# Post-norm attention with product-key experts on one core: another order of preparation, attention outputs paired, 24 maxima ahead instead of 28, one norm two maxima later

## The chip, the core and the metric

The kernel runs on one core of a Trainium2 chip. Its engines work side by side and wait for one another through semaphores: PE (TensorE) multiplies matrices, DVE (VectorE), ACT (ScalarE) and POOL (GpSimd) work elementwise, and SP (SyncE) issues all of the DMAs here, on one queue. The metric is device time in microseconds (us), the median of some runs. The profiled execution is one further run with its own time.

## What is computed

Cut to what matters, for 4 sequences ("batches") of 512 tokens, width 128, 16 heads of width 8, 32 experts:

```python
q, k, v = split_heads(x @ Wq), split_heads(x @ Wk), split_heads(x @ Wv)
attn = softmax(q @ k.T * e ** -0.5) + rel_table[rel_index].reshape(h, s, s)   # per head
x = layernorm(x + (layernorm_1e-3(attn @ v) * gamma + beta))
sim = (x @ hasher_w.T) @ keys.T
vals, idx = top_k(sim, 4);  w = softmax(vals)
o = sum_k w_k * (silu(x @ values_down[idx_k]) @ values_up[idx_k])
out = layernorm(x + (x + o * scale))
```

## The kernel before, in words

**Exactness by pieces.** Queries and keys are needed more exactly than bf16 holds, so each is split into three bf16 pieces (`parts`: high, middle, low). The high one is a copy of the product, `resid` is what is left of it, the middle one a copy of `resid`, the low one `resid` minus the middle one. The pieces go to DRAM (`write_parts`, six DMAs for a batch) and come back as stacks of 72 rows per head (`load_slice`, two DMAs for a group of four heads), `q_stack` and `k_stack`. A score is then one matmul over the 128 rows of both stacks.

**Softmax shift.** The shift of each query, the negative maximum of its row of scores, must be known before the exponentials. For a head and a chunk of 128 queries PE computes scores into one of two banks `sm_ps` (L1003), DVE reduces them (`maximum`, L746). I call the pair "a maximum". There are 64 for a batch, 16 for a group of four heads. When the 16 of a group are done, POOL splits them in three (`split_shift`, L392 to L399), PE turns them (job `shift1` and so on), ACT copies them to `shift_rows` and one DMA lays them into rows 96 to 98 of `q_stack` (`load_shift`).

**Rounds and positions.** Round t (0 to 3) does attention of batch t in 16 positions u, four to a group of heads. A position holds four scores matmuls (L1014), four exponentials on ACT (L645), four maxima for a position 7 ahead (`LEAD`), and the products with the values of the position before (L1027, four per position, stationary `v_cur`). In rounds 1 to 3 the norms, the routing and the experts of batch t-1 are done between them, in rounds 2 and 3 the last part (`up`) of batch t-2 too, and a tail without attention follows.

**Who orders the work.** Nobody plans it: the order of each engine is written out by hand. The table `JOBS` gives for each position the jobs that PE does before and behind its last score; ACT, with `copies`, follows the same table, and DVE has its own places (u, s), where s counts the four maxima of a position. Each engine runs its own list in order and stops at the first wait that isn't met.

**Outputs.** After the four positions of a group, ACT copies the bank `ov_ps` to `o_sb` (`o_copy`), PE turns it by four transposes (jobs `o0` to `o3`, L1032), and DVE divides by the sums (`attend`: a reciprocal at L765 and a multiplication at L767). A head's weights in `v_cur` are 32 columns wide, of which 8 hold values, one holds ones for the sum, and the others zeros.

**Preparation.** `prep(b)` does the transposes of x, the products with the three weights, with three banks of PSUM. PE does `prep(0)` to `prep(2)`, then two maxima, then `prep(3)`, the tables of the relative bias and 28 maxima in all (`EARLY`) between them before round 0.

Of the kernel before, what the change touches and what calls it, by code (L numbers as in the profile page):

```python
# [5 lines left out]
def bass_postln_attention_product_key_ffn(nc, x, w_q, w_k, w_v, rel_table, gamma, beta,  # L6
# [16 lines left out]
    FJ = NE // NJ  # L23
    TOPK = 4
# [5 lines left out]
    EARLY = LEAD * C  # L30
# [16 lines left out]
    with ctx:  # L47
# [36 lines left out]
        rsum = sb("rsum", [P, C, J])  # L84
# [35 lines left out]
        consts_made, stack_set = sem("consts_made"), sem("stack_set")  # L120
# [5 lines left out]
        first_split, mid_made, low_made = sem("first_split"), sem("mid_made"), sem("low_made")  # L126
# [22 lines left out]
        def maxima_of(u, more):  # L149

            return [(u + LEAD, c) for c in range(C) if more or u + LEAD < U]

        JOBS = {0: (["up0", "up1"], ["o3"]), 1: (["up2", "up3"], []), 2: (["shift1", "up4"], ["up5"]),
# [5 lines left out]
        OWN = ("shift0", "shift1", "shift2", "shift3", "o0", "o1", "o2")  # L159
        SPREAD = tuple(f"w{j}" for j in range(FJ))  # L160
        SIDE = ("o0", "x1t", "sim", "o1", "wt", f"up{FJ - 1}") + SPREAD
# [23 lines left out]

        def jobs_of(kind):
            return [n for u in sorted(JOBS) for half in JOBS[u] for n in half if here(n, *kind)]

# [47 lines left out]
        ACT_STEPS = ["tanh0", "sexp"] + [f"tanh{j}" for j in range(1, FJ)]  # L236
# [46 lines left out]
        def _(sp):  # L283
# [35 lines left out]
            def write_parts(b, heads, written):  # L319

                for a in range(2):

                    sp.wait_ge(*((first_split, 2 * a + 2) if b == 0 else (low_made, split_count(b, a))))
# [9 lines left out]
            sp.wait_ge(stack_set, 2)  # L333
# [49 lines left out]
        def _(pool):  # L383
# [17 lines left out]
            def fetch_values(t, g):  # L401

                if not is0(t):

                    pool.wait_ge(pv_done, (t - 1) * U + C * (g + 1))
                    apart(pool)
                nc.gpsimd.tensor_copy(v_cur[:, :, g * J:(g + 1) * J, 0:D],  # L407
                                      v_all[:, :, g * J:(g + 1) * J, t, :]).then_inc(v_ready, 1)
# [59 lines left out]
            nc.gpsimd.memset(q_stack[64:P].bitcast(F32), 0.0).then_inc(stack_set, 1)  # L468
            pool.wait_ge(stack_set, 2)
# [6 lines left out]
            nc.gpsimd.memset(v_cur[:, :, :, D:D + 1], 1.0).then_inc(consts_made, 1)  # L476
            for i in range(PARTS):
                rows = slice(i * NE, (i + 1) * NE)
                pool.wait_ge(consts_made, 8)
                if i:  # L480
                    pool.wait_ge(spread_made, i)
                nc.gpsimd.tensor_copy(spread[rows], ident[rows, rows].rearrange("r (j n) -> r j n", j=FJ).unsqueeze(3)
                                      .to_broadcast([NE, FJ, NJ, PD])).then_inc(spread_made, 1)
            pool.wait_ge(spread_made, PARTS)
# [8 lines left out]
            for g in range(G):  # L493
                fetch_values(0, g)
            low_parts(B - 1)
            split_shift(0, 0)

            def round_(t, attention, experts, more, late):
# [3 lines left out]
                if experts and attention:  # L502

                    pool.wait_ge(misc_done, job(t, "o3", is_kept))
# [55 lines left out]
        def _(act):  # L560
# [3 lines left out]
            def middle_parts(b):  # L564

                for a in range(2):
                    act.wait_ge(resid_made, 2 * b + a + 1)
                    copy(parts[:, b, a, 1, :], resid[:, b % 2, a]).then_inc(mid_made, 1)
# [695 lines left out]
```

## Time and profile before

| | us |
|---|---|
| median of 3 runs (339.32 to 341.76) | 341.53 |
| the profiled execution, its own time | 340.26 |
| its span, first to last instruction | 338.4 |
| PE busy | 303.5 (90%) |
| DVE busy | 237.6 (70%) |
| ACT busy | 202.6 (60%) |
| POOL busy | 127.8 (38%) |
| mean granted clock of TensorE, share of full speed | 0.974 |

The span falls in a preparation of 46.7 us, round 0 (to about 99.8), round 1 (to about 164.5), round 2 (to about 232.7), round 3 (to about 294.1) and a tail of 44.3 us. Busy time of PE overlaps itself, since matmuls are pipelined: a matmul with 512 columns in bf16 shows 380 ns, and the next one can start 0.22 us after it. An engine's idle time counts only where another one waits for what comes late. A row of the timeline may merge neighbours of one kind (x4), and some that overlap a cut are shown twice.

### The profile page before, as it was taken

What the parts mean: (1) busy time and instruction counts of PE and PEld (TensorE: products, weight loads), DVE (VectorE), ACT (ScalarE), POOL (GpSimd) and SP (SyncE); (2) the same over time, 40 slices, a digit from 0 to 9 for tenths busy, and PEclk for the clock granted to TensorE, in tenths of its full rate; (3) what the DMA queues carried; (4) which work ended last, traced back from release to release, by engine and by line L of the source; (5) the groups of instructions that cost most, each with busy time, mean ns of one, the idle gap of its engine ahead of it and who ended that gap; (6) DMA issues with size and microseconds to landing.
All of it is one profiled execution on the core that took longest, in us unless ns stands there. A gap on an engine that the chain in (4) does not pass through costs nothing. (4 is left out here: it accounts for less than half of the span.)

```text
span 338.4 us, 5001 instructions
## 1 busy us (share of the span) xinstructions
PE 303.5 (90%) x1671; PEld 127.8 (38%) x1671; DVE 237.6 (70%) x525; ACT 202.6 (60%) x396; POOL 127.8 (38%) x204
## 2 busy tenths in 40 slices
PE   4859989999999799999998999999989999768890
PEld 2534332332232243333653433335544332465280
DVE  0836897888789869878568798786677922275733
ACT  2544266676776667798455677985556799502600
POOL 8975100100106621164355511653555026324121
PEclk9998999999999999999999999999999999995997
DMA  5486970279520202020202130202001000001001
GB/s 158 104 244 161 302 196 4 71 264 287 153 71 3 71 4 71 1 70 6 69 1 70 35 70 2 73 1 72 1 0 35 0 2 2 0 2 31 0 0 31
DMA packets 28230, 23.17 MB, mean 68 GB/s; under 512 B 6526, under 2 KB 26670, under 8 KB 28206
## 3 DMA queue, kind: packets, MB, share of 16 engines
q1 hardware_dynamic: 28206, 22.87, 24.6%
q8 instruction: 13, 0.21, 0.3%
q14 instruction: 11, 0.09, 0.1%
HBM read 12.18 MB, written 10.52 MB: 67 GB/s over the span
## 5 line engine op out<-in xcount | busy, mean ns | idle before, releaser
L746 DVE TENSOR_REDUCE neg_max<-sm_ps 128x1 f32<-128x512 f32 x256 | 167.8, 684 | 44.9 <-PE sm_ps L1003 43.9
L645 ACT ACTIVATE probs<-st_ps 128x512 f32<-128x512 f32 x256 | 138.4, 612 | 43.0 <-PE st_ps L1014 43.0
L1003 PE MATMUL sm_ps<-k_stack,q_stack 96*128 96x512 bf16 x256 | 98.3, 385 | 9.4 <-DVE neg_max L746 4.5
L1014 PE MATMUL st_ps<-q_stack,k_stack 128*128 128x512 bf16 x256 | 86.3, 380 | 0.7 <-ACT probs L645 0.7
L1027 PE MATMUL ov_ps<-probs,v_cur 128*32 128x512 f32 x512 | 68.2, 605 | 0.5 <-ACT probs L645 0.5
L1003 PEld LDWEIGHTS sm_ps<-k_stack,q_stack 96*128 96x128 bf16 x256 | 24.6, 97 | 103.3 <-DVE neg_max L746 84.7
L435 POOL TENSOR_TENSOR hid<-hid,w_rows 128x512 f32<-128x512 f32 x26 | 33.1, 1273 | 39.1 <-ACT w_rows L562 33.7
L1014 PEld LDWEIGHTS st_ps<-q_stack,k_stack 128*128 128x128 bf16 x256 | 25.3, 99 | 24.9 <-ACT probs L645 6.8
L1048 PEld LDWEIGHTS si_ps<-up_sb,hid 128*128 128x128 f32 x256 | 30.6, 192 | 1.0
L1048 PE MATMUL si_ps<-up_sb,hid 128*128 128x128 f32 x256 | 31.0, 276 | 0.0
L1108 PE MATMUL mi_ps<-x_t,down_sb 128*128 128x512 f32 x48 | 24.8, 598 | 0.3 <-ACT shift_rows L562 0.3
L801 DVE SCALAR_TENSOR_TENSOR hid<-tanh_sb,mi_ps 128x512 f32<-128x512 f32 x24 | 16.3, 681 | 12.1 <-ACT tanh_sb L682 12.1
L682 ACT ACTIVATE tanh_sb<-mi_ps 128x512 f32<-128x512 f32 x24 | 14.6, 608 | 10.4 <-PE mi_ps L1108 10.1
L407 POOL COPY v_cur<-v_all 128x128 f32<-128x128 f32 x16 | 4.5, 289 | 41.1 <-PE ov_ps L1027 41.1
L1027 PEld LDWEIGHTS ov_ps<-probs,v_cur 128*32 128x32 f32 x512 | 10.1, 108 | 22.6 <-issue 17.1
L392 POOL CAST shift_parts<-neg_max 128x16 bf16<-128x16 f32 x16 | 3.1, 196 | 39.9 <-DVE neg_max L746 28.5
L562 ACT ACTIVATE w_rows<-si_ps 128x512 f32<-128x512 f32 x24 | 15.2, 632 | 1.7 <-PE si_ps L1113 1.7
L562 ACT ACTIVATE o_sb<-ov_ps 128x512 f32<-128x512 f32 x16 | 9.7, 606 | 5.3 <-PE ov_ps L1027 5.1
L777 DVE BATCH_NORM_STATS2 stats<-z 128x6 f32<-128x128 f32 x32 | 7.5, 281 | 6.7 <-POOL z L520 6.7
L416 POOL TENSOR_SCALAR veps<-mv 128x4 f32<-128x4 f32 x8 | 1.8, 225 | 26.8 <-DVE mv L786 19.3
L562 ACT ACTIVATE x_t<-si_ps 128x512 f32<-128x512 f32 x4 | 2.4, 598 | 14.7 <-PE si_ps L1032 14.7
L1108 PE MATMUL st_ps<-x_t,down_sb 128*128 128x512 f32 x16 | 10.2, 782 | 0.3 <-DVE hid L801 0.3
(143 smaller groups left out, 295.1 us busy)
## 6 DMA issues: line engine op xcount, KB each, us to landing
stack_dram<-parts SPq DMA_DIRECT2D x18, 384.0 KB, 4.4
q_stack<-stack_dram SPq DMA_DIRECT2D x16, 288.0 KB
k_stack<-stack_dram SPq DMA_DIRECT2D x16, 288.0 KB
stack_dram<-parts SPq DMA_DIRECT2D x6, 288.0 KB, 5.0
x_sb<-L_attn_x SPq DMA_DIRECT2D x4, 256.0 KB, 3.2
out<-y_out SPq DMA_DIRECT2D x4, 256.0 KB, 2.5
stack_dram<-parts SPq DMA_DIRECT2D x6, 96.0 KB, 2.0
down_sb<-L_ffn_values_down SPq DMA_DIRECT2D x1, 512.0 KB, 7.6
```

Source lines behind the costliest of these rows:

```text
L435: nc.gpsimd.tensor_tensor(hid[:, j], hid[:, j], w_rows[:, j], ALU.mult).then_inc(weighed, 1)
L562: return nc.scalar.activation(dst, src, ACT.Copy, scale=scale)
L645: nc.scalar.activation(probs[:, u % 2, j, :], st_ps[:, score_bank(u * J + j), :], ACT.Exp, scale=SCORE_SCALE).then_inc(probs_ready, 1)
L682: nc.scalar.activation(tanh_sb[:, j % 3, :], down_bank(t, j), ACT.Tanh, scale=0.5).then_inc(act_step, 1)
L746: nc.vector.tensor_reduce(neg_max[:, g % 2, col:col + 1], sm_ps[:, c % 2, :], AX.X, ALU.max, negate=True).then_inc(max_ready, 1)
L777: i = nc.vector.bn_stats(into[:, c, :], src[:, c, :])
L801: nc.vector.scalar_tensor_tensor(out=hid[:, j], in0=tanh_sb[:, j % 3, :], scalar=1.0, in1=down_bank(t, j), op0=ALU.add, op1=ALU.mult).then ...
L1003: nc.tensor.matmul(sm_ps[:, c % 2, :], q_stack[0:SHIFT_ROW, h, c * P:(c + 1) * P], k_stack[0:SHIFT_ROW, h, :], start=True, stop=True).then ...
L1014: nc.tensor.matmul(st_ps[:, score_bank(k), :], k_stack[:, g * J + j, kc * P:(kc + 1) * P], q_stack[:, g * J + j, :], start=True, stop=True ...
L1027: i = nc.tensor.matmul(ov_ps[j * TILE:(j + 1) * TILE, :], v_cur[:, kc, g * J + j, :], probs[:, u % 2, j, :], start=(kc == 0), stop=(kc == ...
L1048: i = nc.tensor.matmul(si_ps[:, c * P:(c + 1) * P], hid[:, j, c * P:(c + 1) * P], up_sb[:, j, :], start=(j == 0 and c == 0), stop=(j == FJ ...
L1108: i = nc.tensor.matmul(down_bank(t, j), down_sb[:, j * NJ:(j + 1) * NJ, :], x1_t[:], start=True, stop=True)
```

## The change

Five things change.

1. **Preparation.** DVE clears the lower half of `q_stack` (POOL did). The middle pieces of batch 0 are made by ACT (DVE did), and both low ones follow on DVE. The remainders of batch 3 are copied by ACT and subtracted by POOL (DVE subtracted them straight from PSUM). POOL makes `spread` at its end of the preparation. PE does the transposes of batch 3 ahead of its first two maxima.
2. **SP's queue.** The first `load_shift` goes ahead of `gamma`, `scale` and the pieces of batch 1.
3. **Pairs.** Groups 2n and 2n+1 share one accumulation in `ov_ps`: the even group has values in columns 0 to 7 and the sum in 8, the odd one in 16 to 23 and 24. There are 2 output jobs for a batch, `o0` at position 8 and `o1` in the next round's position 0, for 4 before. `attend` has one reciprocal of 128x32 and two multiplications.
4. **24 maxima ahead.** The positions 0 to 3 of round 0 hold five maxima each.
5. **Round 1.** The statistics of the second norm stand two maxima later, and `x1t` stands in position 6 ahead of `shift2`, with `sim` behind the last score.

The order of PE in the preparation, from the third `prep` on (`x_sb` is the input, `sm_ps` a maximum). Before:

```order
L976 MATMUL st_ps<-ident,x_sb 128x128 x4
L985 MATMUL st_ps<-x_t,wq_sb 128x512
L986 MATMUL st_ps<-x_t,wk_sb 128x512
L990 MATMUL st_ps<-wv_sb,x_t 128x128 x4
L1003 MATMUL sm_ps<-k_stack,q_stack 128x512 x2
L976 MATMUL ov_ps<-ident,x_sb 128x128 x4
L1003 MATMUL sm_ps<-k_stack,q_stack 128x512
L985 MATMUL mi_ps<-x_t,wq_sb 128x512
L986 MATMUL si_ps<-x_t,wk_sb 128x512
```

And now:

```order
L997 MATMUL st_ps<-ident,x_sb 128x128 x4
L1006 MATMUL st_ps<-x_t,wq_sb 128x512
L1009 MATMUL st_ps<-x_t,wk_sb 128x512
L1013 MATMUL st_ps<-wv_sb,x_t 128x128 x4
L997 MATMUL ov_ps<-ident,x_sb 128x128 x4
L1026 MATMUL sm_ps<-k_stack,q_stack 128x512 x2
L1006 MATMUL mi_ps<-x_t,wq_sb 128x512
L1026 MATMUL sm_ps<-k_stack,q_stack 128x512
L1009 MATMUL si_ps<-x_t,wk_sb 128x512
```

The transposes of batch 3 have moved ahead of the first two maxima, and one maximum stands between its two products.

SP's queue at the same place, behind the loads of the last slice (`shift_rows` is the shift of group 0). Before:

```order
L339 DMA gamma_sb<-L_attn_gamma 128x128
L340 DMA scale_sb<-L_ffn_scale 128x1
L327 DMA stack_dram<-parts 384x1x512 x3
L327 DMA stack_dram<-parts 128x1536 x3
L298 DMA q_stack<-shift_rows 3x16x128
L343 DMA down_sb<-L_ffn_values_down 128x32x32
```

And now:

```order
L307 DMA q_stack<-shift_rows 3x16x128
L350 DMA gamma_sb<-L_attn_gamma 128x128
L351 DMA scale_sb<-L_ffn_scale 128x1
L336 DMA stack_dram<-parts 384x1x512 x3
L336 DMA stack_dram<-parts 128x1536 x3
L353 DMA down_sb<-L_ffn_values_down 128x32x32
```

The shift has moved ahead of eight DMAs. The expert loads stand ahead of the shift of group 1, as before.

DVE in round 1, from the first norm's last step to the routing's first. Before:

```order
L786 BN_AGGR mv<-stats 128x2 x4
L746 TENSOR_REDUCE neg_max<-sm_ps 128x1 x7
L777 BN_STATS stats<-z 128x6 x2
L746 TENSOR_REDUCE neg_max<-sm_ps 128x1
L777 BN_STATS stats<-z 128x6 x2
L746 TENSOR_REDUCE neg_max<-sm_ps 128x1
L786 BN_AGGR mv<-stats 128x2 x4
L746 TENSOR_REDUCE neg_max<-sm_ps 128x1 x2
L765 RECIPROCAL rsum<-si_ps 128x16
L767 TENSOR_TENSOR attn<-si_ps,rsum 128x4x32
L746 TENSOR_REDUCE neg_max<-sm_ps 128x1 x7
L863 MAX top<-sim 128x8 x4
```

And now:

```order
L808 BN_AGGR mv<-stats 128x2 x4
L769 TENSOR_REDUCE neg_max<-sm_ps 128x1 x9
L799 BN_STATS stats<-z 128x6 x2
L769 TENSOR_REDUCE neg_max<-sm_ps 128x1
L799 BN_STATS stats<-z 128x6 x2
L769 TENSOR_REDUCE neg_max<-sm_ps 128x1
L808 BN_AGGR mv<-stats 128x2 x4
L769 TENSOR_REDUCE neg_max<-sm_ps 128x1 x8
L885 MAX top<-sim 128x8 x4
```

Nine maxima stand ahead of the statistics instead of seven, and the output's two instructions are gone from here (they come at position 10).

The diff, cut to its core:

```diff
-    EARLY = LEAD * C
+    EARLY = (LEAD - 1) * C
...
-        def maxima_of(u, more):
+        def maxima_of(t, u, more):
+            if t == 0 and u < C:
+                return [divmod(k, C) for k in range(EARLY + u * (C + 1), EARLY + (u + 1) * (C + 1))]
             return [(u + LEAD, c) for c in range(C) if more or u + LEAD < U]
-        JOBS = {0: (["up0", "up1"], ["o3"]), 1: (["up2", "up3"], []), 2: (["shift1", "up4"], ["up5"]),
-                3: (["up6"], ["up7"]), 4: ([], ["o0"]), 5: ([], ["x1t"]),
-                6: (["shift2", "sim"], ["down0"]), 7: ([], ["down1"]), 8: ([], ["o1", "down2"]),
+        JOBS = {0: (["up0", "up1"], ["o1"]), 1: (["up2", "up3"], []), 2: (["shift1", "up4"], ["up5"]),
+                3: (["up6"], ["up7"]), 4: ([], []), 5: ([], ["x1t"]),
+                6: (["shift2", "sim"], ["down0"]), 7: ([], ["down1"]), 8: ([], ["o0", "down2"]),
...
-                12: (["w2"], ["down6", "w3"]), 13: (["w4"], ["down7", "w5"]), 14: (["shift0", "w6"], ["o2"]),
+                12: (["w2"], ["down6", "w3"]), 13: (["w4"], ["down7", "w5"]), 14: (["shift0", "w6"], []),
+        SHORT_JOBS = {**JOBS, 5: ([], []), 6: (["x1t", "shift2"], ["sim", "down0"])}
...
+            load_shift(0, 0)
             sp.dma_start(gamma_sb[:], bass.AP(gamma.tensor, 0, [[0, P], [1, E]])).then_inc(rows_loaded, 16)
             sp.dma_start(scale_sb[:], bass.AP(ffn_scale.tensor, 0, [[0, P], [1, 1]])).then_inc(rows_loaded, 16)
             write_parts(1, slice(0, H), parts_written[1])
-            load_shift(0, 0)
...
+            for a in range(2):
+                pool.wait_ge(last_copied, a + 1)
+                nc.gpsimd.tensor_sub(resid[:, 1, a], resid[:, 1, a], parts[:, B - 1, a, 0, :]).then_inc(last_resid, 1)
+            split_shift(0, 0)
             low_parts(B - 1)
-            split_shift(0, 0)
+            for i in range(PARTS):
...
                     copy(parts[:, b, a, 0, :], made).then_inc(prep_copied, 1)
+                    if b == B - 1:
+                        act.wait_ge(low_made, split_count(b - 2, a))
+                        copy(resid[:, 1, a], made).then_inc(last_copied, 1)
+                if b == 0:
+                    middle_parts(0)
...
-                    if u == 7 and experts:
+                    if u == 8 and experts:
                         act.wait_ge(pool_step, pool_at(t - 1, "sdiff"))
...
+            nc.vector.memset(q_stack[64:P].bitcast(F32), 0.0).then_inc(rows_cleared, 1)
...
-                        nc.vector.tensor_copy(parts[:, b, a, 1, :], resid[:, 0, a]).then_inc(first_split, 1)
...
-                nc.vector.reciprocal(rsum[:], o[:, :, :, D]).then_inc(rsum_ready, 1)
-                dve.wait_ge(rsum_ready, n + 1)
...
+                nc.vector.reciprocal(rsum[:], o[:, :, :, :, D]).then_inc(rsum_ready, 1)
+                dve.wait_ge(rsum_ready, t * PAIRS + n + 1)
+                for k in range(2):
+                    g = 2 * n + k
+                    i = nc.vector.tensor_tensor(attn[:, :, g * J * D:(g + 1) * J * D].rearrange("p c (j d) -> p c j d", d=D),
+                                                o[:, :, :, k, 0:D], rsum[:, :, :, k].unsqueeze(3).to_broadcast([P, C, J, D]),
+                                                ALU.mult)
...
-                elif at == ((3, 1) if late else (4, 0)):
+                elif at == ((3, 1) if late else (4, 2)):
...
-                        if attention and s == 0 and u in (5, 9, 15):
+                        if attention and (u, s) == (10, 1):
...
                 for j in range(J):
                     i = nc.tensor.matmul(ov_ps[j * TILE:(j + 1) * TILE, :], v_cur[:, kc, g * J + j, :],
-                                         probs[:, u % 2, j, :], start=(kc == 0), stop=(kc == C - 1))
+                                         probs[:, u % 2, j, :], start=(g % 2 == 0 and kc == 0),
+                                         stop=(g % 2 == 1 and kc == C - 1))
```

## Rows read from the trace of the kernel before

**Rows 1.** The page, part 1 and part 5 (columns: busy us, mean ns, idle before).

```profile
PE 303.5 (90%) x1671; PEld 127.8 (38%) x1671; DVE 237.6 (70%) x525; ACT 202.6 (60%) x396; POOL 127.8 (38%) x204
...
L562 ACT ACTIVATE o_sb<-ov_ps 128x512 f32<-128x512 f32 x16 | 9.7, 606 | 5.3 <-PE ov_ps L1027 5.1
```

**Rows 2.** Windows by stage: busy time per engine, PE's clock, DMA share, GB/s.

```profile
46.70:99.80 53.10, 52.62 (x281) 15.22 (x279) 43.83 (x75) 38.07 (x76) 4.42 (x20) 1.00 0.47 143
99.80:164.50 64.70, 62.14 (x334) 22.40 (x334) 52.74 (x115) 46.73 (x94) 26.53 (x44) 1.00 0.17 41
164.50:232.70 68.20, 66.67 (x381) 28.25 (x380) 54.15 (x123) 46.93 (x92) 29.75 (x48) 1.00 0.16 40
```

**Rows 3.** Timeline of the first 19 us: start, length, engine, line, tiles, idle before.

```profile
9.10 1.64 DVE L730 CAST parts<-resid 128x512 bf16<-128x512 f32 x1
10.77 0.69 DVE L732 TENSOR_TENSOR parts<-resid,parts 128x512 bf16<-128x512 f32 x1
11.49 4.36 SPq L327 DMA_DIRECT2D stack_dram<-parts  x6
11.82 3.65 POOL L482 CAST spread<-ident 32x1024 bf16<-32x1024 f32 x3
13.17 1.40 DVE L732 TENSOR_TENSOR parts<-resid,parts 128x512 bf16<-128x512 f32 x1
15.56 3.72 POOL L489 TENSOR_TENSOR x_sb<-x_sb,beta_sb 128x512 f32<-128x512 f32 x3
16.04 1.13 PE L985 MATMUL st_ps<-x_t,wq_sb 128*128 128x512 f32 x2 [0.74 <-ACT x_t L562]
```

**Rows 4.** Timeline from 22 us to the first scores.

```profile
22.49 0.60 PE L1003 MATMUL sm_ps<-k_stack,q_stack 96*128 96x512 bf16 x2 [3.57 <-DMA k_stack<-stack_dram]
29.63 0.63 PE L1032 MATMUL st_ps<-ident,rel_win 128*128 128x128 f32 x4 [0.30 <-issue]
31.53 6.46 SPq L327 DMA_DIRECT2D stack_dram<-parts  x6
31.55 7.80 DVE L746 TENSOR_REDUCE neg_max<-sm_ps 128x1 f32<-128x512 f32 x12
39.26 0.21 PE L1032 MATMUL mi_ps<-ident_bf,shift_parts 128*128 128x128 bf16 x1 [0.63 <-POOL shift_parts L399]
44.90 0.60 ACT L562 ACTIVATE bias_v<-st_ps 128x512 f32<-128x512 f32 x1 [0.45 <-PE st_ps L1032]
```

**Rows 5.** Windows of the same stretch, columns as in Rows 2.

```profile
22.48:28.90 6.42, 6.12 (x21) 3.20 (x22) 2.58 (x4) 2.83 (x5) 4.43 (x7) 0.73 0.65 218
28.90:46.70 17.80, 15.46 (x112) 6.41 (x111) 15.57 (x25) 6.96 (x15) 3.10 (x6) 1.00 0.98 262
```

**Rows 6.** DMA issues: name, count, size, us from issue to landing.

```profile
up_sb<-L_ffn_values_up SPq DMA_DIRECT2D x1, 512.0 KB, 9.3
...
gamma_sb<-L_attn_gamma SPq DMA_DIRECT2D x1, 64.0 KB, 8.8
```

**Rows 7.** Timeline of round 0, at the end of group 0.

```profile
58.04 2.48 DVE L746 TENSOR_REDUCE neg_max<-sm_ps 128x1 f32<-128x512 f32 x4 [0.61 <-PE sm_ps L1003]
61.49 0.65 PE L1032 MATMUL si_ps<-ident,o_sb 128*128 128x128 f32 x4
61.98 0.38 PE L1014 MATMUL st_ps<-q_stack,k_stack 128*128 128x512 bf16 x1
...
63.44 0.25 DVE L765 RECIPROCAL rsum<-si_ps 128x16 f32<-128x16 f32 x1
63.72 0.29 DVE L767 TENSOR_TENSOR attn<-si_ps,rsum 128x128 f32<-128x128 f32 x1
```

**Rows 8.** Timeline of PE in rounds 1 and 2, where it stood idle.

```profile
114.07 0.39 PE L1003 MATMUL sm_ps<-k_stack,q_stack 96*128 96x512 bf16 x1 [1.19 <-DVE neg_max L746]
118.97 0.63 PE L1032 MATMUL si_ps<-ident,x 128*128 128x128 f32 x4 [0.91 <-POOL x L425]
180.09 0.39 PE L1003 MATMUL sm_ps<-k_stack,q_stack 96*128 96x512 bf16 x1 [0.72 <-DVE neg_max L746]
```

More of the change, by code:

```diff
@@ L184, in here, with jobs_at @@
             return (late if n[:2] == "up" else attention if n in OWN else experts) and (more or n != "shift0")
+        def jobs_at(kind, u):
+            return (SHORT_JOBS if kind == SECOND else JOBS).get(u, ([], []))
         def jobs_of(kind):
-            return [n for u in sorted(JOBS) for half in JOBS[u] for n in half if here(n, *kind)]
+            return [n for u in range(U) for half in jobs_at(kind, u) for n in half if here(n, *kind)]
         def job(t, name, counted):
@@ L235, in bass_postln_attention_product_key_ffn @@
         LATE_POOL = ["ceps", "ccentre", "cpow"]
-        ACT_STEPS = ["tanh0", "sexp"] + [f"tanh{j}" for j in range(1, FJ)]
+        ACT_STEPS = ["tanh0", "tanh1", "sexp"] + [f"tanh{j}" for j in range(2, FJ)]
         def dve_at(f, name):
@@ L406, in fetch_values @@
                     apart(pool)
-                nc.gpsimd.tensor_copy(v_cur[:, :, g * J:(g + 1) * J, 0:D],
+                first = HALF_TILE * (g % 2)
+                nc.gpsimd.tensor_copy(v_cur[:, :, g * J:(g + 1) * J, first:first + D],
                                       v_all[:, :, g * J:(g + 1) * J, t, :]).then_inc(v_ready, 1)
@@ L475, in _ @@
             nc.gpsimd.tensor_copy(ident_bf[:], ident[:]).then_inc(consts_made, 1)
[L476 to L484, printed above, removed]
+            for half in range(2):
+                sums = v_cur[:].rearrange("p c (n k j) w -> p c n k j w", n=PAIRS, k=2)[:, :, :, half]
+                last = HALF_TILE * half + D
+                for n in range(PAIRS):
+                    i = nc.gpsimd.memset(sums[:, :, n, :, last:last + 1], 1.0)
+            i.then_inc(consts_made, 1)
             pool.wait_ge(beta_loaded, 16)
@@ L693, in round_ @@
                 for u in range(U):
-                    before, behind = JOBS.get(u, ([], []))
+                    before, behind = jobs_at((attention, experts, more, late), u)
                     if attention:
@@ L839, in expert_steps @@
                 if at == (1, 0):
-                    attend(f, G - 1, t)
+                    attend(f, PAIRS - 1, t)
                     if not attention:
@@ L922, in round_ @@
                 for u in range(U):
-                    maxima = maxima_of(u, more) if attention else []
+                    maxima = maxima_of(t, u, more) if attention else []
                     for s in range(C):
-                        if s < len(maxima):
-                            maximum(t, *maxima[s])
-                        if attention and s == 0 and u in (5, 9, 15):
-                            g = {5: 0, 9: 1, 15: 2}[u]
-                            attend(t, g, t)
+                        for pos_c in maxima[s:s + 1] if s < C - 1 else maxima[s:]:
+                            maximum(t, *pos_c)
+                        if attention and (u, s) == (10, 1):
+                            attend(t, 0, t)
                         if late and attention:
@@ L1021, in values @@
                     pe.wait_ge(v_ready, t * G + g + 1)
-                    if not (is0(t) and g == 0):
-                        pe.wait_ge(o_copied, t * G + g)
+                    if g % 2 == 0 and not (is0(t) and g == 0):
+                        pe.wait_ge(o_copied, t * PAIRS + g // 2)
                 pe.wait_ge(probs_ready, J * n + J)
@@ L1071, in misc @@
                         pe.wait_ge(hidden_made, hidden_count(f, int(last[4:])))
+                    elif last == name and t == B:
+                        pe.wait_ge(hidden_made, hidden_count(f - 1, FJ - 1))
                 elif int(name[4:]) >= 3:
@@ L1121, in early_maxima @@
                         maximum_scores(0, *early.pop(0))
-            for b in range(B - 1):
+            for b in range(B):
                 prep(b)
-            early_maxima(2)
-            prep(B - 1)
             early_maxima(2)
@@ L1200, in round_ @@
                 for u in range(U):
-                    before, behind = JOBS.get(u, ([], []))
+                    before, behind = jobs_at(kind, u)
                     if not attention and u == 0:
                         before, behind = behind, before
-                    todo = maxima_of(u, more) if attention else []
+                    todo = maxima_of(t, u, more) if attention else []
                     def maxima(k):
-                        for pos_c in todo[k:k + 1]:
+                        for pos_c in todo[k:k + 1] if k < C - 1 else todo[k:]:
                             maximum_scores(t, *pos_c)
@@ L1215, in score @@
                                 scores(t, u, j)
-                    spread = not any(here(n, *kind) and n[:2] in ("do", "up") for n in JOBS.get(u - 1, ([], []))[1])
+                    spread = not any(here(n, *kind) and n[:2] in ("do", "up") for n in jobs_at(kind, u - 1)[1])
                     score(*range(1 + spread))
```

91 lines of the change are left out of this document (48 added, 43 removed).

## The prediction

> **What bounds the kernel now.** I read the page first: PE is busy 90% of the span, DVE 70%, ACT 60% [rows 1]. Then the windows by stage, since a share of the whole says nothing about a stage: in round 0 PE is busy 52.6 of 53.1 us, in round 1 62.1 of 64.7, in round 2 66.7 of 68.2, with its clock at full speed, 2.4 GHz [rows 2]. So in the rounds what counts is what PE must do and the few places where it waits. A plain position of round 0 is shared, though: DVE needs 2.48 us for its four maxima and idles 0.61 us while PE is at the value products, 3.09 us together [rows 7]. Neither can shorten it alone, and a fifth maximum lengthens it. Last, the timeline of the preparation, which is a chain and no throughput: pieces of batch 0, their write, their load, the first maximum at 22.49 us [rows 3, 4].
>
> **The preparation, step by step.** The sum is made against the profiled execution, 340.26 us (span 338.4).
>
> *First write.* SP issues the first three DMAs at 11.49 and the other three when the second low piece is ready, at 13.17 + 1.40 = 14.57; all are issued at 15.85, so three take 1.28 us [rows 3]. ACT takes over the middle pieces, which is 0.60 us each there [rows 1] for 1.64 us of a cast on DVE [rows 3]. Then the second low piece is ready at about 12.9 and the queue is free at 12.77: gain 1.7 us. The floor is 1.0 us, if a subtraction is held up once more, the ceiling 1.8 us (the queue). ACT's two copies, 0.60 us each, come ahead of the copies that `prep(1)` waits for, so batches 1 and 2 move some 0.65 us back. That hides behind the load's way, since PE waited 3.57 us for it [rows 4].
>
> Here the trace and a rule differ a little. A low piece's subtraction took 0.69 us beside POOL's memsets and 1.40 us beside its cast of `spread` [rows 3]. The new place is beside POOL's additions of beta, of 1.24 us each [rows 3]; I take 0.69 and 1.40 once more. The Trainium skill, SBUF — State Buffer, section Who interferes with whom, says that a DVE instruction with two SBUF inputs is held off by a GpSimd instruction that reads SBUF, for all of its length. By that rule both could wait for an addition, and the sum below would be some 0.7 us higher.
>
> *Batch 3.* PE stood still for 3.57 us before the first maximum, and in the 6.42 us after it its clock was 0.73 of full: part of it at half speed, 1.2 GHz [rows 4, 5]. Now the transposes of batch 3 fill most of the wait: PE's idle there shrinks to under 1 us and I expect no fall. The first maximum comes at 22.49 - 1.7 = 20.8. From it to the table transposes there were 29.63 - 22.49 = 7.1 us. Now there are six maxima at 0.22, two products of about 1.1 us at full clock [rows 3], the values' 1.1, and ACT's copy of it, some 4.7 us: the table comes at 25.5, a gain of 4.1 us (the 1.7 in it). Floor 2.5 us, if the clock falls all the same.
>
> *Shift of group 0.* DVE had done 6 maxima when its run of 12 in 7.80 us began at 31.55; the 16th was its tenth, at 38.0, and PE turned the shift at 39.26 [rows 4]. Without the last two subtractions on DVE it has 8 behind it at 27.5 and does the other 8 at 0.62 to 0.65 us by 33. The turn comes 1.3 us later, at 34.3: gain 5.0 us. POOL's two new subtractions (1.2 us each by the additions [rows 3]) are over by then, and it makes the last low pieces and `spread` (3.65 us [rows 3]) behind it, where nobody asks until round 1.
>
> *First scores.* Before they came at 46.7, behind four last maxima at 0.62 us each. These are gone, but the last bias copy, which PE waits for, ended at 45.5 [rows 4], so no more than 1.1 us is gained: scores at 40.6, **-6.1 us** in all (floor -3.5, ceiling -7). The shift's DMA, now ahead of `gamma`, has 5 us to land.
>
> **Round 0.** 16 maxima are now spread as 20 over four positions, 0.60 to 0.62 us for each extra: **+2.4 us** (ceiling; the floor is +0.9, four times PE's 0.22, if DVE's idle 0.61 took them in, but that idle lies around the value products and a maximum behind the fourth doesn't reach it). An output job costs PE 61.98 - 61.49 = 0.49 us and DVE about as much (0.25 and 0.29), and a position with one is about 0.4 us longer [rows 7]. There were three; there is one, with one more multiplication of 0.29: -0.55 us. **Round 0: +1.9 us.**
>
> **Round 1.** PE waited 1.19 us for DVE, which stood at the second norm's statistics, and 0.91 us at `x1t` for POOL [rows 8]. Two maxima later in the order DVE comes there about when POOL's result is ready, and `x1t` behind another position meets its input: -2.1. `sim` then stands only two short matmuls behind `x1t`, and must wait for ACT's copy of 0.60 us: +0.4. Two output jobs fewer, 0.44 us each on a busy PE, are -0.9, and position 8 to 9, where DVE is late, gives 0.2: **-2.8 us.** POOL's chain from `attend` to the first norm doesn't move; it starts 0.25 us later by the longer `attend`.
>
> **Rounds 2 and 3.** Their norms stay where they were; the wait at the statistics, 0.72 us [rows 8], hangs on POOL and grows by 0.25. Two output jobs and a piece of DVE's load are gone in each: -1.25 + 0.25 = **-1.0 us each**. In the second half of round 3 ACT carries the experts' copies too, and loses one of 0.60 us: **-0.4 us.**
>
> **Tail.** It waits for `attend` from its start: one multiplication more, **+0.3 us**. The rest of its 44.3 us has the same instructions.
>
> Costed at nothing: the clearing of `q_stack` on DVE (DVE has nothing to do before the first subtraction, which comes ahead of the 9.10 of its cast [rows 3]); the eight copies that ACT loses in the middle rounds (it idles between exponentials there); the exponential of the routing one position later, whose reader comes another position behind. If ACT became late, that last one would cost its 0.33 us.
>
> **Sum:** -6.1 + 1.9 - 2.8 - 1.0 - 1.0 - 0.4 + 0.3 = -9.1, so 340.26 - 9.1 = 331.2 us. The median of the runs shown is 1.3 us above that execution; I forecast a median of **332 us**.
>
> **The rivals.**
>
> *A, the start is bound by its DMAs (time 335.5, chance 0.2).* The DMA share from 28.9 to 46.7 was 0.98 [rows 5], `gamma` took 8.8 us to land behind the slices [rows 6]. If the slice of group 1 lands no earlier than before, the maxima from the 17th on wait. The same would hold if ACT, which waits for `scale` ahead of the first exponential, gets it late: it is now issued at about 36.5. Then the start gives 2.5 us instead of 6.1. Against it: the chain that fills the queue starts 1.7 us earlier as a whole, and the write of batch 1 moves out of the way.
>
> *B, the expert loads hold the shift of group 1 (334, chance 0.1).* SP now issues the write of batch 1 behind the first shift: some 34.8 + 0.9 for the shift, 1.4 for `gamma` and `scale`, 6.46 for the six writes [rows 4], so it comes to `down` and `up` at 43.5, and `up`, issued right behind `down`, took 9.3 us to land [rows 6]: 53 to 53.5. The shift of group 1 is behind both in the queue, and PE needs it at 40.6 + 4 x 3.09 + 4 x 0.6 - 0.6 = 54.8. The margin is 1 to 2 us; if it's eaten up, about 2 us are lost.
>
> *C, more than forecast (328.5, chance 0.1).* All waits of the rounds fall together: the fifth maxima cost 0.9 and the late rounds give 2 us each.
>
> *D, no change to measure (338.5 to 341, chance 0.05).* The order of the preparation doesn't do what it says: the first write gains nothing, since the landing rather than the issue decides, and the clock falls as before. Then only the rounds are left: about -3, less what A takes.
>
> *E, slower (344, chance 0.03): PE at half clock in the first four positions of round 0.* After the 3.57 us of idleness the clock was at half for a part of the next 6.42 us [rows 4, 5]. If it fell once more at the start of round 0, where PE now does 3.0 us of work in 3.7, a position would take some 6.6 us, 3 more each, and the gain of 9.1 turns to +3. It decides if the window of these positions shows a clock of 0.5. Against it: the same engine ran rounds 0 to 3 at 1.00 with waits of up to 1.19 us in them [rows 2, 8]. The Trainium skill, TensorE: Matmul & The Clock Gate, What's actually happening, has the clock follow how busy PE has been lately; by it such a fall could be, and the trace at these shares speaks against it.
>
> My forecast has the rest, 0.52, with a range of its own of 330 to 334.5.
>
> **Range and chances.** 328.5 to 337 us takes in the forecast, A, B and C, and leaves D and E out, with tails of the others. A measurement of this kernel tells a change of 1% (3.4 us) from none. Faster by over 1%, that is below 338.1: the forecast, A, B, C, 0.92. Within 1%: 0.05. Slower by over 1%: 0.03.
>
> **What would show it.** In the windows: the first scores at 40 to 41.5 us and a clock near 1.00 from 20 to 29 us; positions of 3.7 us four times, then 3.1; round 0 of about 55 us; in round 1 no wait of PE at DVE's statistics or at `x1t`, and one of about 0.4 at `sim`; rounds 2 and 3 each 1.0 to 1.4 us shorter; tail 44.6. The prediction is wrong if the first scores stay above 43 us, if a half-clock window stands in round 0, or if the fifth maximum costs much less or more than 0.6.

## The result, and the profile after

The changed kernel ran in 338.59 us (median of 20 executions, 336.26 to 341.6), the kernel before beside it in 340.57 (20 executions). The ratio is 0.9932, with a 95% interval of 0.9915 to 0.9949; it leaves out two slow executions of the changed kernel (341.32 and 341.6). So the gain is real and small, 0.7%, which is within the 1% called no change, and far from the 332 us forecast. 338.59 lies above the range (328.5 to 337) too.

The profiled execution took 337.84 us against 340.26 (spans 336.0 and 338.4), so 2.4 us less, where 9.1 were predicted. First, on the page, the busy time of each engine [rows 1 for before]:

```profile
PE 300.0 (89%) x1639; PEld 124.1 (37%) x1639; DVE 235.6 (70%) x514; ACT 200.9 (60%) x392; POOL 126.1 (38%) x208
```

The shares are those of before to a point. Where the time went is told by the windows by stage of the changed kernel (from, to, length, then busy time and count of PE, PEld, DVE, ACT, POOL, PE's clock, DMA share, GB/s), to be held against [rows 2]. A round's border is, as there and to 0.1 us, the start of the fourth exponential of its first position. Round 0 begins with its first scores, and the tail with the turn of the last output (288.9 here, 293.6 before, where the prediction's tail of 44.3 us began at 294.1):

```profile
41.70:96.40 54.70, 52.86 (x276) 14.77 (x276) 44.58 (x74) 37.11 (x74) 4.45 (x20) 1.00 0.62 181
96.40:160.20 63.80, 61.86 (x326) 21.29 (x325) 52.38 (x113) 45.79 (x91) 26.58 (x44) 1.00 0.18 41
160.20:228.20 68.00, 65.89 (x374) 27.13 (x373) 53.94 (x121) 46.01 (x90) 29.81 (x48) 1.00 0.16 40
228.20:288.90 60.70, 56.70 (x321) 21.72 (x319) 34.60 (x90) 43.38 (x86) 27.98 (x40) 1.00 0.02 6
288.90:336.00 47.10, 31.02 (x172) 22.16 (x172) 25.41 (x84) 7.63 (x14) 11.56 (x18) 0.85 0.04 11
```

The last two of before, not shown yet:

```profile
232.70:293.60 60.90, 57.24 (x329) 22.70 (x326) 35.00 (x92) 44.20 (x88) 27.96 (x40) 1.00 0.02 6
293.60:338.40 44.80, 30.34 (x172) 21.74 (x172) 25.10 (x83) 7.63 (x14) 11.54 (x18) 0.84 0.04 12
```

By stage, predicted and measured, in us:

```
start            -6.1   -5.0   (46.7 -> 41.7)
round 0          +1.9   +1.6   (53.1 -> 54.7)
round 1          -2.8   -0.9
round 2          -1.0   -0.2
round 3          -1.4   -0.2
tail             +0.3   +2.3   (44.8 -> 47.1)
```

Two readings in this already point to the cause. In round 2 PE's busy time fell by 66.67 - 65.89 = 0.78 us, two output jobs less, but the round by only 0.2 to 0.3: PE idles more. And the tail, costed at +0.3, is the largest miss of a single stage.

**Start.** The timeline of the changed kernel (start, length, engine, line, what, idle before and who ended it) has the new chain [rows 3, 4 for before]; SPq is the queue of SP:

```profile
10.53 1.47 DVE L755 TENSOR_TENSOR parts<-resid,parts 128x512 bf16<-128x512 f32 x2
...
11.44 3.52 SPq L336 DMA_DIRECT2D stack_dram<-parts  x6
...
21.46 0.61 PE L1026 MATMUL sm_ps<-k_stack,q_stack 96*128 96x512 bf16 x2 [1.74 <-DMA k_stack<-stack_dram]
...
28.87 6.64 DVE L769 TENSOR_REDUCE neg_max<-sm_ps 128x1 f32<-128x512 f32 x10 [0.85 <-PE sm_ps L1026]
...
35.42 0.22 PE L1057 MATMUL mi_ps<-ident_bf,shift_parts 128*128 128x128 bf16 x1 [0.64 <-POOL shift_parts L409]
...
41.72 0.60 PE L1037 MATMUL st_ps<-q_stack,k_stack 128*128 128x512 bf16 x2 [0.69 <-ACT bias_v L579]
```

The low pieces are ready at 12.0, earlier than the 12.9 estimated, but the six issues now take 3.52 us back to back and end at 14.96, 0.9 us earlier than before; the first maximum comes 1.03 us earlier, where 1.7 was taken. The fourth issue begins at 13.44, behind the first three, so that a piece that is ready sooner doesn't help. The gap of 0.85 us in DVE's maxima, waiting for PE, was not in the working; the shift is turned at 35.4 rather than 34.3. From the turn to the scores it is 6.30 us, against 46.72 - 39.26 = 7.46, and the scores wait for the bias copy: the 1.1 us of the last step was right.

The two subtractions for the low pieces took 1.47 us together here. That is not always so. In experiment 3, whose code up to this place is the same, the rows are

```profile
10.57 2.35 DVE L753 TENSOR_TENSOR parts<-resid,parts 128x512 bf16<-128x512 f32 x2
10.71 1.67 POOL L493 TENSOR_TENSOR x_sb<-x_sb,beta_sb 128x512 f32<-128x512 f32 x1 [1.26 <-PE ov_ps L995]
```

POOL's addition of beta, 1.27 us by itself, came in between and took 1.67, and the second subtraction took 1.57 for 0.69. So it was in six of the ten profiled executions with the new preparation (0.68 and 1.57 to 1.63 us), near the 0.69 and 1.40 that the prediction took. That both wait, the case it set beside its sum, came in none: the first subtraction always began ahead of the addition. The longer second one cost next to nothing, since the last pieces, at 12.8 to 13.1, were still ahead of the queue's fourth issue at 13.4 or later: the first maximum came at 21.72 us on average in these six and at 21.62 in the other four.

**Round 0.** DVE's row of one of the four positions with five maxima reads:

```profile
47.47 3.12 DVE L769 TENSOR_REDUCE neg_max<-sm_ps 128x1 f32<-128x512 f32 x5 [0.57 <-PE sm_ps L1026]
```

3.12 + 0.57 = 3.69 us, with DVE's idle still there [rows 7]: a fifth maximum costs its full 0.6.

**Tail.** `sexp` is the exponential of the routing, `wexp` its first reader on DVE, `hid` are products with the experts' first matmuls (`down`). First the kernel before, in which `wexp` finds its input ready (no idle stands in its row); DVE's and ACT's timeline, then PE's wait at `down`:

```profile
309.65 0.47 DVE L863 MAX8 top<-sim 128x8 f32<-128x32 f32 x4 [3.80 <-ACT sim L562]
...
312.59 0.29 DVE L892 TENSOR_TENSOR wexp<-sexp,mask 128x128 f32<-128x128 f32 x1
...
311.10 0.60 ACT L682 ACTIVATE tanh_sb<-st_ps 128x512 f32<-128x512 f32 x1 [1.59 <-PE st_ps L1108]
311.59 0.30 ACT L705 ACTIVATE sexp<-sdiff 128x128 f32<-128x128 f32 x1
...
314.66 1.12 PE L1108 MATMUL st_ps<-x_t,down_sb 128*128 128x512 f32 x2 [0.28 <-DVE hid L801]
```

The same places in the changed kernel:

```profile
304.85 0.47 DVE L885 MAX8 top<-sim 128x8 f32<-128x32 f32 x4 [3.38 <-ACT sim L579]
...
308.90 0.29 DVE L914 TENSOR_TENSOR wexp<-sexp,mask 128x128 f32<-128x128 f32 x1 [1.15 <-ACT sexp L728]
...
306.30 0.60 ACT L705 ACTIVATE tanh_sb<-st_ps 128x512 f32<-128x512 f32 x1 [1.59 <-PE st_ps L1137]
308.00 0.60 ACT L705 ACTIVATE tanh_sb<-st_ps 128x512 f32<-128x512 f32 x1 [1.11 <-PE st_ps L1137]
308.50 0.30 ACT L728 ACTIVATE sexp<-sdiff 128x128 f32<-128x128 f32 x1
...
310.97 1.33 PE L1137 MATMUL st_ps<-x_t,down_sb 128*128 128x512 f32 x2 [1.90 <-DVE hid L823]
```

`sexp` stands behind the second `tanh` on ACT, and that one waits 1.11 us for PE's `down`. DVE waits 1.15 us at `wexp`, its `hid` products queue behind, and PE waits 1.90 us, for 0.28 before, for a bank that `hid` frees.

### The profile page after: what moved, and what is told of

Same layout as the page of the kernel before. It is cut to its first block and busy times, and to the rows that moved or that the text cites. A ratio compares the mean times of both kernels' runs of the same rounds, so it can differ in the third digit from the quotient of the medians.

```text
span 336.0 us, 4908 instructions
## 1 busy us (share of the span) xinstructions
PE 300.0 (89%) x1639; PEld 124.1 (37%) x1639; DVE 235.6 (70%) x514; ACT 200.9 (60%) x392; POOL 126.1 (38%) x208
## 5 line engine op out<-in xcount | busy, mean ns | idle before, releaser
L446 POOL TENSOR_TENSOR hid<-hid,w_rows 128x512 f32<-128x512 f32 x26 | 33.1, 1275 | 41.2 <-ACT w_rows L579 34.3
L1137 PE MATMUL st_ps<-x_t,down_sb 128*128 128x512 f32 x16 | 11.1, 842 | 1.9 <-DVE hid L823 1.9
L705 ACT ACTIVATE tanh_sb<-st_ps 128x512 f32<-128x512 f32 x8 | 4.8, 597 | 7.9 <-PE st_ps L1137 7.9
```

The lines of the kernel that those rows point to most:

```text
L446: nc.gpsimd.tensor_tensor(hid[:, j], hid[:, j], w_rows[:, j], ALU.mult).then_inc(weighed, 1)
L705: nc.scalar.activation(tanh_sb[:, j % 3, :], down_bank(t, j), ACT.Tanh, scale=0.5).then_inc(act_step, 1)
L1137: i = nc.tensor.matmul(down_bank(t, j), down_sb[:, j * NJ:(j + 1) * NJ, :], x1_t[:], start=True, stop=True)
```

## Experiments

Each is a small edit to one of the two kernels. "Mark" is the start of the fourth exponential of the first position of round 0, 48.96 us before and 43.98 in the changed kernel. "Tail" is from here on the time from the start of the last exponential of attention to the end, 47.25 us before and 49.62 in the changed kernel. Every kernel has one profiled execution, from which marks and tails are taken.

**1. The tail's exponential back.** In the tail alone; the count of ACT's steps follows it.

```diff
-                    if u == 8 and experts:
+                    if u == (8 if attention else 7) and experts:
```

> The changed kernel, but in the tail the routing exponential stands ahead of tanh1 on ACT again. Theory 1 (the exponential's place is what lengthened the tail): the tail, 47.05 us from the output turn to the end of the span, is back at 44.7 to 45.1, DVE's wexp waits under 0.3 us instead of 1.15, PE waits under 0.6 us at down3 instead of 1.90 and its clock falls once, not twice; all stages before it stand within 0.1 us; median 338.6 - 2.2 = 336.4. Rival (the longer attend at its start, or the clock by itself): the tail stays at 46.5 to 47.1 and the median at 338.6.

Measured: 336.83 us (ratio 0.9898, 0.9857 to 0.994). From the mark to the last exponential of attention it is the same to 0.02 us. DVE's wait is gone, and PE's is 0.76:

```profile
307.18 0.30 ACT L729 ACTIVATE sexp<-sdiff 128x128 f32<-128x128 f32 x1
...
308.18 0.29 DVE L915 TENSOR_TENSOR wexp<-sexp,mask 128x128 f32<-128x128 f32 x1
...
310.25 1.13 PE L1138 MATMUL st_ps<-x_t,down_sb 128*128 128x512 f32 x2 [0.76 <-DVE hid L824]
```

The tail is 48.68 us, against 49.62 changed and 47.25 before. From MAX8 to `wexp` it is 2.94 us as before; the changed kernel has 4.05. So the 1.1 us came back, but only 0.9 of the tail's 2.4, less than expected: PE still waited 0.76 and the clock still fell a second time, later. The median is 1.8 us less.

**2. The same edit alone, in the kernel before.**

```diff
-        ACT_STEPS = ["tanh0", "sexp"] + [f"tanh{j}" for j in range(1, FJ)]
+        ACT_STEPS = ["tanh0", "tanh1", "sexp"] + [f"tanh{j}" for j in range(2, FJ)]
...
-                    if u == 7 and experts:
+                    if u == 8 and experts:
```

> The kernel before with this one edit: the routing exponential stands behind tanh1 and one position later in all rounds and in the tail. Theory 1: tail 44.76 -> 46.8 to 47.1 us, half clock in a second stretch of the tail, rounds 0 to 3 unchanged within 0.2 us; median 340.6 + 2.2 = 342.8. Rival (the exponential only hurts together with the new attend): tail within 0.3 us of 44.76, median 340.6.

Measured: 344.11 us, ratio 1.0114 (1.008 to 1.0147). The rounds stand within 0.04 us, and the tail is 50.07 for 47.25, +2.8. The same two waits are there:

```profile
314.49 0.29 DVE L892 TENSOR_TENSOR wexp<-sexp,mask 128x128 f32<-128x128 f32 x1 [1.15 <-ACT sexp L705]
...
316.55 1.12 PE L1108 MATMUL st_ps<-x_t,down_sb 128*128 128x512 f32 x2 [1.42 <-DVE hid L801]
```

So the exponential by itself makes the longer tail. The median rose by 3.7 us. In the profiled execution, 3.6 us longer, another 0.7 stood at its start (mark 49.66), which this edit does not touch, with a longer half-clock stretch there.

**3. All 28 early maxima.**

```diff
-    EARLY = (LEAD - 1) * C
+    EARLY = LEAD * C
...
-            if t == 0 and u < C:
-                return [divmod(k, C) for k in range(EARLY + u * (C + 1), EARLY + (u + 1) * (C + 1))]
```

> The changed kernel with all 28 early maxima ahead of the first scores, so no position with five. Theory 1 (a fifth maximum costs its whole 0.6 us wherever DVE is the longer engine, and ahead of the scores a maximum costs as much as in a position): first four positions 2.4 us shorter, first scores 1.9 to 2.5 us later than 41.7, end within 0.5 us of the changed kernel, 338.6. Rival (PE waits for a bias copy and not for DVE's maxima ahead of the first scores, as the prediction had it): first scores at most 1.1 us later, end 1.3 us earlier, 337.3. Second rival: 28 cost more there than 2.4, end later.

Measured: 336.95 us (ratio 0.9897, 0.9867 to 0.9927), mark at 45.20, the first four positions in 12.38 us for 14.78. The rival holds: -2.4 for +1.2. Over the profiled executions with the new preparation and no clock fall in it the mark is 44.25 on average with 24 (three) and 45.32 with 28 (five): 1.1 us, what the prediction took for the bias copy. So to have 24 early maxima instead of 28 costs 2.4 - 1.1 = 1.3 us.

**4. The norm of round 1 back.**

```diff
-        SHORT_JOBS = {**JOBS, 5: ([], []), 6: (["x1t", "shift2"], ["sim", "down0"])}
+        SHORT_JOBS = JOBS
...
-                elif at == ((3, 1) if late else (4, 2)):
+                elif at == ((3, 1) if late else (4, 0)):
```

The two steps behind it go back likewise, and the routing's first step on DVE by one place.

> The changed kernel with the jobs and the statistics of the second norm of round 1 where they were before. Round 1 took 63.8 us against 64.7 before; predicted were 61.9. Theory 1 (the move takes away PE's waits of 1.19 and 0.91 us, but most comes back as new waits in positions 6 to 8 and 10): round 1 is 0.3 to 0.9 us longer than in the changed kernel. Rival (the move gives its full 1.7 us and the paired outputs take it back): round 1 is 1.5 to 1.9 us longer. Second rival (the move gives nothing): within 0.2 us. Other rounds unchanged.

Measured: 339.58 us (ratio 0.9982, 0.9955 to 1.0009). Round 1 takes 64.81 us for 63.80: the move is worth 1.0 us, just above theory 1 and far under the rival, and the medians differ by 1.0 as well. Positions 4 and 5 gain 1.46 + 0.79 = 2.2 us (predicted 2.1), position 6 gives 0.9 back and 7 another 0.3. The wait of 0.4 predicted at `sim` isn't in PE's rows; a wait at the turn of the next shift is, behind the norm on POOL:

```profile
117.37 0.22 PE L1057 MATMUL mi_ps<-ident_bf,shift_parts 128*128 128x128 bf16 x1 [0.48 <-POOL shift_parts L409]
```

**5. `attend` at position (9,0).**

```diff
-                        if attention and (u, s) == (10, 1):
+                        if attention and (u, s) == (9, 0):
```

> The changed kernel with DVE's attend of the paired output at position (9,0) in place of (10,1). Theory 1 (at position 10 PE's wt waits 0.40 us for the later and longer attend): that wait goes and position 10 is 0.4 us shorter in rounds 1 and 2 and 0 to 0.4 in round 3; position 9 is 0 to 0.3 longer; each of these rounds 0.1 to 0.4 us shorter. Rival (DVE is the longer engine in this stretch whatever the order): the 0.4 us moves to position 9 or 11 and the rounds stay within 0.1 us.

One execution, 338.37 us. The wait it aimed at was this one of the changed kernel, and DVE's work behind it:

```profile
135.44 0.42 PE L1057 MATMUL si_ps<-ident_bf,w_parts 128*96 128x128 bf16 x4 [0.40 <-DVE attn L788]
...
134.51 0.35 DVE L784 RECIPROCAL rsum<-si_ps 128x32 f32<-128x32 f32 x1
134.89 0.49 DVE L788 TENSOR_TENSOR attn<-si_ps,rsum 128x128 f32<-128x128 f32 x2
```

It goes, and position 10 is 0.43 us shorter in rounds 1 to 3. But in rounds 1 and 2 position 8 grows by 0.40 and 9 by 0.22, so they are 0.18 longer each, and round 0 is 0.14 longer; only round 3 gains, 0.44. Theory 1 fails in rounds 1 and 2: as the rival has it, the 0.84 us of work on DVE takes its cost along, and a little more.

**6. The paired outputs alone, in the kernel before.** Besides the new bank layout, the core is

```diff
-                        if attention and s == 0 and u in (5, 9, 15):
-                            g = {5: 0, 9: 1, 15: 2}[u]
-                            attend(t, g, t)
+                        if attention and (u, s) == (10, 1):
+                            attend(t, 0, t)
```

> The kernel before with the paired outputs alone. Predicted were -0.55 us in round 0, -0.9 to -1.1 in round 1, -1.25 + 0.25 in each of rounds 2 and 3, +0.3 in the tail, in all some -3.5. Theory 1 (most of an output job lay under DVE's floor, and the later attend makes new waits): round 0 -0.6 to -0.75 (16 maxima in 12 positions then), round 1 0 to +0.3, round 2 and round 3 -0.2 to -0.3 each, tail +0.3 to +0.9; median 340.4 to 340.9. Rival (the pairs give what was predicted and other parts of the change took it back): rounds 1 to 3 together -2.5 or more, median 337.5.

Measured: 339.87 us, ratio 0.9982 (0.9962 to 1.0003). By stage: round 0 -0.72, round 1 +0.14, round 2 -0.27, round 3 -0.24. Its windows of rounds 1 and 2:

```profile
99.10:163.90 64.80, 61.45 (x325) 21.25 (x325) 52.44 (x113) 45.87 (x91) 26.52 (x44) 1.00 0.16 40
163.90:231.90 68.00, 65.89 (x373) 27.14 (x372) 53.94 (x121) 46.04 (x90) 29.75 (x48) 1.00 0.16 40
```

Against [rows 2] PE has 0.69 and 0.78 us less to do (0.88 predicted), DVE only 0.30 and 0.21, and the rounds keep their length to 0.3 us. Positions 8, 9 and 14, and 5 in rounds 2 and 3, gain 0.1 to 0.2 each where they gain, position 10 loses 0.43 to the wait shown above (round 3 has it back in position 11), and in round 1 position 1 loses 0.23.

Position 4 in rounds 2 and 3 takes 4.02 us with the output job and without it, and the rows of round 2 show why. PE before:

```profile
183.36 0.60 PE L1032 MATMUL si_ps<-ident,o_sb 128*128 128x128 f32 x4
...
185.10 0.39 PE L1003 MATMUL sm_ps<-k_stack,q_stack 96*128 96x512 bf16 x1 [0.27 <-DVE neg_max L746]
```

and with the pairs:

```profile
183.64 0.38 PE L1011 MATMUL sm_ps<-k_stack,q_stack 96*128 96x512 bf16 x1 [0.25 <-DVE neg_max L753]
...
184.53 0.39 PE L1011 MATMUL sm_ps<-k_stack,q_stack 96*128 96x512 bf16 x1 [0.30 <-DVE neg_max L753]
```

The output job, 0.44 us of PE, is gone, and PE waits for DVE 0.55 us instead of 0.27. DVE's maxima, with the statistics of the late norm between them, begin 0.35, 1.33 and 2.21 us into the position in both kernels. PE's last maximum hangs on them, then its value products, then the next position's scores. The job had stood in time in which PE would have waited.

**7. The new preparation alone.** The changed preparation, with 28 early maxima, in the kernel before.

> The kernel before with the new preparation alone (28 early maxima, all else as before). Theory 1 (start and rounds don't touch each other): first exponential group of round 0 at 45.2 us where the clock does not fall at the start and some 2 us later where it does, against 48.96 before; rounds and tail within 0.2 us of before; median 340.4 - 3.7 = 336.7. Rival (the gain of the start is partly given back in round 0 by the expert loads or the second shift, now issued against another traffic): round 0 longer than 50.83 by over 0.3 us.

Measured: 337.17 us, ratio 0.9894 (0.9865 to 0.9923). Mark 45.13 for 48.96, rounds within 0.01 us of before. Theory 1 holds. This part alone does at least as well as the whole change (0.9932; the intervals overlap a little).

**8. Three mends together** (1, 3 and 5).

> The changed kernel with the three mends together: the routing exponential ahead of tanh1 in the tail, 28 early maxima, attend at position (9,0). By theory 1: -1.5 for the exponential, -1.3 for the early maxima, -0.3 x 3 for attend = -3.7 against the changed kernel: median 334.9, ratio to the kernel before 0.984. Rival (what ends the tail is how the clock falls there, and it takes each gain back): 336 to 337.

Measured: 334.69 us, ratio 0.9828 (0.98 to 0.9855). The 334.9 expected is met by luck, for the parts are others. Against the changed kernel the profiled execution has -1.1 us for the early maxima (-1.3 expected), +0.1 in the four rounds together for `attend` (-0.9 expected), and -2.1 in the tail (-1.5 expected), in which the clock had no second fall.

**9. `shift2` of round 1 behind the scores.**

```diff
-6: (["x1t", "shift2"], ["sim", "down0"])
+6: (["x1t"], ["shift2", "sim", "down0"])
```

> The changed kernel with PE's shift2 of round 1 behind the scores of position 6, where it stood ahead of them. In the changed kernel the moved norm took 2.24 us off positions 4 and 5 of round 1 and gave 0.89 + 0.34 back at 6 and 7. Theory 1 (0.48 us of this is PE's wait for POOL's shift_parts, which comes behind the last scaling of the norm): position 6 0.3 to 0.5 us shorter, round 1 63.3 to 63.5 instead of 63.80. Rival (DVE sets the pace of positions 6 and 7, with four maxima and the statistics' rest): the wait goes, but the time stays within 0.1 us.

One execution, 338.73 us. The wait is gone, position 5 is 0.42 us shorter and 6 is 0.30 longer, the round 63.67 for 63.80. The rival comes nearer: of the 0.48 us wait only 0.13 was time.

**10 and 11. The best places together.** Mends 1 and 3 with `attend` at (9,0) in round 3 alone, then with 9 added.

> The changed kernel with the routing exponential ahead of tanh1 in the tail, 28 early maxima, and attend at position (9,0) in round 3 alone. Against the same with attend at (9,0) in all rounds (334.69): rounds 1 and 2 0.18 us shorter each, round 0 0.14, so 334.2, ratio to the kernel before 0.981. Rival (the gains of the rounds are under what the clock in the tail makes of them): 334.7 or more.

> The kernel of the run before this one with shift2 of round 1 behind the scores of position 6. Theory 1: another 0.4 us in round 1, 333.8. Rival: no difference, 334.2.

Measured: 335.38 (0.9848, 0.9812 to 0.9884) and 335.83 us (0.9871, 0.9838 to 0.9904). The four rounds together are 0.50 and 0.65 us shorter than those of experiment 8, but the medians are not shorter: executions of one kernel differ by more (3.4 us in experiment 10). Experiments 8, 10 and 11 all beat both kernels, and these runs don't rank them.

## Why the prediction was wrong

The direction held, the size didn't: -9.1 predicted, -2.4 in the profiled execution, 6.7 us missing. By the prediction's own steps:

- **Paired outputs, 3.1 us missing.** The step "Two output jobs fewer, 0.44 us each on a busy PE" and its like for rounds 2 and 3 gave -1.1 - 1.0 - 1.4 = -3.5 us in rounds 1 to 3; alone they gave +0.14 - 0.27 - 0.24 = -0.4 (experiment 6). PE's saved time is real, but there most of it becomes idle time, as position 4 shows. Only in round 0, with little else to do, is a job its price (-0.72; predicted -0.55). I read "PE busy 62 of 65 us" as "PE is the bound", though round 0 had just been shown to be shared. The job's place in the position was missing from the working, and so was that PE's turn of `w_parts` (`wt`, the routing weights) waits for `attend` at its new place (0.43 us in each of three rounds).
- **The exponential, about 2 us missing.** It stood under "costed at nothing", with 0.33 us if ACT became late. The cover named, a reader one position later, exists in the rounds (unchanged in experiment 2) and not in the tail, where the same order of steps runs with no maxima between. Experiments 1 and 2 show it from both sides: from MAX8 to `wexp` 2.94 us in all executions with the early exponential and 4.05 with the late one (3.56 in experiment 5, where PE's `down` ran at the full clock), and 0.9 and 2.8 us at the end. Over all thirteen profiled executions the tail is 47.93 us on average with the early one (seven) and 49.77 with the late (six): 1.8 us. How much of it the exponential itself costs, beyond the 1.1, and how much the second fall of the clock, wasn't separated. The `attend` of +0.3 is there too: from the output turn to MAX8 it is 16.01 us before and 16.31 with pairs alone, with a clock that fell 4 to 6 us ahead of MAX8; where it fell 3 us ahead of it, 15.56 without pairs (experiment 7) and 15.86 to 15.90 with them.
- **The start, 1.1 us missing.** The first write gave 1.0 for 1.7. The step that failed is "the queue is free at 12.77": it gave the first three issues the 1.28 us of the last three, but they took 2.0 us (11.44 to 13.44), and the queue, not the second piece, became the limit. And the ten maxima of DVE began 0.85 us late for want of scores. The floor of 3.5 holds.
- **The norm of round 1, 0.7 us missing.** The two waits went as predicted (2.2 for 2.1), but 1.2 us came back in the next two positions where 0.4 were taken. One place is POOL's next shift, which comes behind the norm's last scaling, but experiment 9 shows that it accounts for 0.13 us; that the rest is DVE's pace is argued, not shown.
- **Round 0, right.** +1.6 for +1.9; the fifth maxima cost +2.4, as predicted. What the working didn't do is hold them against the 1.1 us that they buy at the start, both numbers of which stood in it.

Of the rivals, A didn't come: `gamma` landed in 3.4 us for 8.8 and the round's first scores waited for a bias copy. B neither: no wait at the shift of group 1. E neither, the clock is 1.00 in all rounds. D, with a chance of 0.05, has the measured 338.59 in its times, but by luck: its reasons, a first write that gains nothing and a clock that falls as before, didn't come. No rival had the case that PE's saved work turns into idle time. A warning stood in the numbers: a round 1 of 64.7 - 2.8 = 61.9 us would have left PE, busy 61.86 us in it now, no idle time at all.

The numbers of the other middle positions stay partly open. That `attend` costs time in rounds 1 and 2 at either of two places is shown (experiment 5), and what holds position 4 at 4.02 us in rounds 2 and 3 is read from rows (experiment 6), but no run took work from DVE in rounds 1 to 3 to see them get shorter.

## What to carry to other kernels

An engine that is busy 96% of a stage isn't its bound where another takes turns with it: cost the removal of its work position by position, by what that position waits for last, and take what is saved as idle time until a row says otherwise. When a table of steps is used by several stages, cost a reordering in each, above all in the one with least other work. And hold the two sides of a trade against each other: the 24 early maxima bought 1.1 us with 2.4.

## What the runs showed of the hardware

**Much of the scatter goes with the clock.** In the profiled executions with the old preparation PE's clock fell to half in the start in 3 of 3, with the new one in 2 of 10, where PE's wait for the stacks is 1.4 to 2.3 us instead of 3.1 to 3.6. It did not fall in experiment 11, whose wait was the longest of the new ones, 2.25 us, and it did in experiment 4 with 1.98. These are the windows around it in the changed kernel and in that of experiment 4, of the same code at the start (columns as in the windows by stage):

```profile
21.40:28.00 6.60, 5.87 (x28) 3.28 (x28) 5.23 (x8) 3.80 (x10) 5.08 (x8) 1.00 0.66 213
```

```profile
21.50:28.00 6.50, 6.12 (x21) 3.12 (x22) 3.50 (x6) 2.77 (x5) 4.86 (x8) 0.74 0.65 212
```

At 0.74, PE gets through 21 matmul records where at 1.00 it gets through 28, and the mark comes at 45.8 (46.0 in experiment 5, the other one with a fall) for 44.0 to 44.4. The prediction's "under 1 us of idleness and no fall" was wrong in the wait and right in most executions about the fall.

In the tail the clock fell in every one. Besides the last 2 to 6 us of the program, which are at half in all of them, the kernel before has one stretch at half, the changed one two (clock 0.67 and 0.85 in the windows below, 0.51 and 0.92 before in 303.8 to 314.2 and what follows):

```profile
301.50:311.70 10.20, 7.53 (x18) 3.86 (x16) 5.43 (x21) 2.86 (x6) 4.79 (x8) 0.67 0.09 26
311.70:336.00 24.30, 15.28 (x85) 10.28 (x84) 10.50 (x25) 4.77 (x8) 4.24 (x5) 0.85 0.04 11
```

Before the second fall PE had waited 1.90 us at `down`; the eight matmuls behind it took 4.88 us, 3.65 before. Experiment 5, with the late exponential too, had no such fall between and has a tail of 48.10 us, where the five others with it have 49.62 to 50.31: the end of this program carries about 2 us of this, and so does any one profile of it. The rounds, all at full clock, agreed to 0.02 us between kernels with the same code in them, which is why one profile of each was enough to price their parts.

**Two engines hold each other up.** In the new preparation POOL's addition of beta took 1.27 us by itself. In all ten profiled executions one of them began while DVE was subtracting a low piece: it took 1.33 to 1.67 us in eight, and 1.27 in two (experiments 1 and 11), where the two overlapped by only 0.1 us. The subtraction took 0.68 to 0.69 us when no addition was under way at its beginning, and 1.57 to 1.63 in the six executions in which one was (1.40 beside the cast of `spread` [rows 3]). In all six it ended 0.54 to 0.56 us behind the addition, so that most of its own 0.69 us lies behind the addition's end.
